# A graph-attention edge pass with each step's relus first on ScalarE, and the projection of step i ahead of the scores of step i-1 on TensorE

## The reference, cut to what matters

```
h = layer_norm(x, ln1_g, ln1_b)
xl, xr = (h @ Wl + bl), (h @ Wr + br)                 # [n, 2 heads, 128]
e = leaky_relu(xl[src] + xr[dst], 0.2)
score = einsum('ehd,hd->eh', e, att)
ex = exp(score - segment_max(score, dst)[dst])
out = segment_sum(xl[src] * (ex / segment_sum(ex, dst)[dst]), dst)
x = x + ((out + gat_b) @ proj_W + proj_b)
h = layer_norm(x, ln2_g, ln2_b)
x = x + (gelu(h @ W1 + b1) @ W2 + b2)
```

## Time and profile before

| | |
|---|---|
| median of three runs | 2266.37 us (2265.63 to 2266.79) |
| span of the profiled execution | 2743.9 us (the page gives no time of this execution beside its span) |
| PE, PE weight loads busy | 72%, 48% |
| DVE, ACT, POOL busy | 47%, 51%, 56% |
| mean granted TensorE clock | 0.891 |

### The profile page before, as it was taken

The page is one execution under the profiler, slowest core; times in us unless marked ns, Lnnn a source line. Parts: engine busy times, 40 slices in busy tenths (PEclk is TensorE's granted clock), DMA queues, the critical chain, the costliest instruction groups (busy, mean ns, idle before and its releaser), DMA issues. The chain is left out here.

```text
span 2743.9 us, 66371 instructions
## 1 busy us (share of the span) xinstructions
PE 1964.3 (72%) x19001; PEld 1307.1 (48%) x19001; DVE 1302.8 (47%) x5318; ACT 1411.6 (51%) x3474; POOL 1543.5 (56%) x1664
## 2 busy tenths in 40 slices
PE   4567777777777777777744777777777777777775
PEld 2234555554554555545533445544545545555453
DVE  7324554554544544544541344444444444444445
ACT  4324555555555555555542455555555555555554
POOL 4656666565566566565315666566556565565540
PEclk9778988989999998998966898999998999889997
DMA  5544444444454454444214444444444444444430
GB/s 133 166 111 127 127 130 128 132 130 128 130 131 128 129 132 129 128 133 128 73 56 117 122 125 128 126 121 129 128 125 128 123 125 127 125 124 128 124 107 7
DMA packets 236750, 332.67 MB, mean 121 GB/s; under 512 B 51011, under 2 KB 160491, under 8 KB 236395
## 3 DMA queue, kind: packets, MB, share of 16 engines
q0 software_dynamic: 75072, 208.30, 29.4%
q1 hardware_dynamic: 161322, 120.16, 14.9%
HBM read 308.02 MB, written 20.25 MB: 120 GB/s over the span
## 5 line engine op out<-in xcount | busy, mean ns | idle before, releaser
L982 POOL DMA_INDIRECT rows<-table,src_t x1564 | 1492.5, 954 | 995.5 <-PE psum L1182 367.9
L1428 DVE SCALAR_TENSOR_TENSOR acc<-acc,keep,psum 128x129 f32 x782 | 273.2, 349 | 1164.2 <-PE psum L1182 596.9
L1207 ACT COPY wgt<-psum 128x256 f32<-128x256 f32 x392 | 146.0, 373 | 1030.2 <-PE psum L1190 649.4
L1089 PE MATMUL psum<-lz,att_w 128*32 128x256 f32 x3128 | 281.2, 434 | 513.6 <-ACT lz L1200 444.6
L1103 PE MATMUL psum<-ident,rows 128*128 128x128 f32 x3128 | 578.4, 315 | 34.9 <-DMA rows<-table,src_t 34.9
L1103 PEld LDWEIGHTS psum<-ident,rows 128*128 128x128 f32 x3128 | 412.3, 160 | 237.5 <-issue 187.8
L1200 ACT ACTIVATE lz<-psum 128x512 f32<-128x512 f32 x782 | 427.8, 603 | 41.0 <-DMA table<-row 14.4
L1182 PE MATMUL psum<-rows,wgt 128*32 128x129 f32 x6256 | 313.8, 302 | 49.3 <-issue 45.9
L1089 PEld LDWEIGHTS psum<-lz,att_w 128*32 128x32 f32 x3128 | 64.4, 113 | 590.0 <-ACT lz L1200 509.4
L1106 PE MATMUL psum<-oh,xrw 96*128 96x256 bf16 x1564 | 344.4, 306 | 0.0
L1279 ACT ACTIVATE ex<-hold_s,peak 128x256 f32<-128x256 f32 x392 | 201.5, 514 | 138.4 <-issue 87.4
(11 more groups left out here) (257 smaller groups left out, 2100.1 us busy)
## 6 DMA issues: line engine op xcount, KB each, us to landing
xrw<-xr_split SPq DMA_DIRECT2D x782, 48.0 KB
relb<-rel_d SPq DMA_DIRECT2D x194, 192.0 KB
rows<-table,src_t POOLq DMA_INDIRECT x1564
relb<-cyc_d SPq DMA_DIRECT2D x194, 64.0 KB
xr_split<-split SPq DMA_DIRECT2D x50, 192.0 KB, 1.9
table<-row SPq DMA_DIRECT2D x50, 130.0 KB, 2.1
x_mid<-x SPq DMA_DIRECT2D x25, 64.0 KB
xo<-x_mid SPq DMA_DIRECT2D x25, 64.0 KB
```

What stands on the lines that cost most here:

```text
L982: pool.indirect_dma_start(rows[:, ring(u), t, u % M, :, :].rearrange("p h c -> p (h c)"), None, s["tables"][layer][0:NP, :], bass.Indirect ...
L1089: m = pe.matmul(out[o:o + W, 0:UE], w["att_w"][:, h * W:h * W + W], lz[:, u % M, h * UE:h * UE + UE], start=False, stop=True, skip_group_c ...
L1428: m = v.scalar_tensor_tensor(a, a, s["keep"][:, u:u + 1], sum_bank(i - 6)[:, c:c + D + 1], ALU.mult, ALU.add)
```

## The change

On ACT, the relus of a step now belong to the units that PE projects in the same step (step i, where it was i-1); they come after the small node work at the head of the step, and ahead of the copy `wgt`, which is now that of step i-4. The exponentials are those of step i-3 and stand ahead of the copy `hold_s`, which is now that of step i-1. On PE, the transposes of `ex` of step i-4 move from the end of the step to its head, `project(i)` comes ahead of `score(i-1)`, and inside `node_work` the combine matmuls (line 1143) come first. The mask product is done in four matmuls of 32 columns where it was two of 64. `lz` has four buffers. DVE's `lowest` is that of step i-2.

```diff
-    lz = sb("lz", [P, M, H * UE], F32)
+    lz = sb("lz", [P, 2 * M, H * UE], F32)
...
                 for u in of_step(g):
-                    at = u % M * HW
-                    pe.matmul(out[at:at + HW, 0:UE], s["mask_w"][:, :], oh[:, u % (3 * M), :],
-                              start=False, stop=False, skip_group_check=True)
+                    for h in range(H):
+                        o = u % M * HW + h * W
+                        pe.matmul(out[o:o + W, 0:UE], s["mask_w"][:, h * W:h * W + W], oh[:, u % (3 * M), :],
+                                  start=False, stop=False, skip_group_check=True)
                 pe.wait_ge(lz_ready, min(g * M + M, NU))
...
-                                      lz[:, u % M, h * UE:h * UE + UE], start=False, stop=True, skip_group_check=True)
+                                      lz[:, u % (2 * M), h * UE:h * UE + UE], start=False, stop=True, skip_group_check=True)
...
             for i in range(END):
+                if of_step(i - 4):
+                    pe.wait_ge(ex_ready, i - 3)
+                    hold(pe, wgt_ready, i - 4)
+                    for t in range(K):
+                        m = pe.transpose(ps[4][:, t * P:t * P + P], ex[:, (i - 4) % 2, t * P:t * P + P],
+                                         s["ident"][:, :])
+                    m.then_inc(ex_turned, 1)
...
+                for u in of_step(i):
+                    project(u)
                 if of_step(i - 1):
                     score(i - 1)
-                for u in of_step(i):
-                    project(u)
                 old = of_step(i - 5)
...
                 node_work(i)
-                if of_step(i - 4):
-                    pe.wait_ge(ex_ready, i - 3)
...
             def relu(u):
 
                 act.wait_ge(z_ready, u + 1)
-                hold(act, score_ready, u // M)
-                act.activation(lz[:, u % M, :], ps[u % M][:, :], ACT.Relu).then_inc(lz_ready, 1)
+                hold(act, score_ready, u // M - 1)
+                act.activation(lz[:, u % (2 * M), :], ps[u % M][:, :], ACT.Relu).then_inc(lz_ready, 1)
 
             for i in range(END):
-                new = of_step(i - 1)
-                if of_step(i - 5):
-                    act.wait_ge(ex_turned, i - 4)
...
-                for u in new:
-                    relu(u)
...
+                for u in of_step(i):
+                    relu(u)
+                if of_step(i - 4):
+                    act.wait_ge(ex_turned, i - 3)
+                    hold(act, sums_ready, i - 5)
+                    act.copy(wgt[:, (i - 4) % 2, :, :].rearrange("p t c -> p (t c)"), ps[4][:, 0:UE]
+                             ).then_inc(wgt_ready, 1)
...
+                old = of_step(i - 3)
+                if old:
+                    n, c = len(old) * HW, (i - 3) % 4
+                    act.wait_ge(max_ready, min(i - 1, NO))
+                    hold(act, ex_turned, i - 4)
...
-                new = of_step(i - 2)
+                new = of_step(i - 1)
                 if new:
                     n = len(new) * HW
-                    act.wait_ge(score_ready, i - 1)
-                    hold(act, ex_ready, i - 5)
...
+                    act.wait_ge(score_ready, i)
+                    hold(act, ex_ready, i - 4)
...
-                if of_step(i - 3):
-                    lowest(i - 3)
+                if of_step(i - 2):
+                    lowest(i - 2)
```

More of the change, by code:

```diff
@@ L1110, in node_work @@
             def node_work(i):
+                for q, tl in [(0, nodes(i, -1)), (1, nodes(i, 0))]:
+                    for t in tl:
+                        pe.wait_ge(staged, t + 1)
+                        if t < NT - 1:
+                            hold(pe, z2_ready if last else xrf_ready, t - 1)
+                        else:
+                            pe.wait_ge(lz_ready, NU)
+                        for m in range(2):
+                            for c in range(3):
+                                mm = pe.matmul(bank(t)[m * HW:m * HW + HW, q * (D + 1):q * (D + 1) + D + 1],
+                                               s["sel"][:, c, :, :].rearrange("p h w -> p (h w)"),
+                                               stg[t % 2][:, 2 * (2 * q + m) + c, :], start=(c == 0),
+                                               stop=(c == 2), skip_group_check=True)
+                        if q == 1:
+                            mm.then_inc(comb_ready, 1)
                 for t in nodes(i, 1):
@@ L1133, in node_work @@
                                   ).then_inc(next_proj, 1)
[L1134 to L1148, removed]
-            for i in range(END):
+            for i in range(END):
+                if of_step(i - 4):
[5 more added lines that the diff above has]
+                    m.then_inc(ex_turned, 1)
                 for t in nodes(i, 5):
@@ L1198, in relu @@
                 act.wait_ge(z_ready, u + 1)
-                hold(act, score_ready, u // M)
-                act.activation(lz[:, u % M, :], ps[u % M][:, :], ACT.Relu).then_inc(lz_ready, 1)
+                hold(act, score_ready, u // M - 1)
+                act.activation(lz[:, u % (2 * M), :], ps[u % M][:, :], ACT.Relu).then_inc(lz_ready, 1)
             for i in range(END):
-                new = of_step(i - 1)
-                if of_step(i - 5):
-                    act.wait_ge(ex_turned, i - 4)
-                    hold(act, sums_ready, i - 6)
-                    act.copy(wgt[:, (i - 5) % 2, :, :].rearrange("p t c -> p (t c)"), ps[4][:, 0:UE]
-                             ).then_inc(wgt_ready, 1)
-                for u in new:
-                    relu(u)
                 for t in nodes(i, 6):
@@ L1267, in _ @@
                     act.activation(am2[:, :], am[t % 2][:, :], ACT.Square).then_inc(sq_ready, 1)
-                new = of_step(i - 2)
+                old = of_step(i - 3)
[3 more added lines that the diff above has]
+                    hold(act, ex_turned, i - 4)
+                    act.activation(ex[0:n, (i - 3) % 2, :], hold_s[0:n, c, :], ACT.Exp, bias=peak[0:n, c:c + 1],
+                                   scale=-1.0).then_inc(ex_ready, 1)
+                new = of_step(i - 1)
                 if new:
                     n = len(new) * HW
-                    act.wait_ge(score_ready, i - 1)
-                    hold(act, ex_ready, i - 5)
[L1273 to L1280, removed]
+                    act.wait_ge(score_ready, i)
+                    hold(act, ex_ready, i - 4)
+                    act.copy(hold_s[0:n, (i - 1) % 4, :], scores(i - 1)[0:n, 0:UE]).then_inc(held, 1)
                 new = of_step(i)
                 if new:
+                    hold(act, score_ready, i - 1)
                     for u in new:
                         act.wait_ge(rows_in[u % ROWS], (u // ROWS + 1) * (16 * K))
-                    hold(act, score_ready, i - 1)
                     act.copy(lin[:, i % 2, :, :].rearrange("p t (c w) -> p (t c) w", w=W),
```

## The result

The changed kernel takes 2208.64 us (median of four runs, 2205.07 to 2211.80) against 2266.58 us of the kernel before: a ratio of 0.9746, with a 95% interval of 0.9729 to 0.9762. The forecast was 2192 us, with POOL's gathers as the bound. The time came out 17 us above the forecast: 58 us were gained where 74 were forecast.

The account below looks back on a forecast made before the run. A loop of waits between PE and ACT bounds the kernel, then POOL's gathers: two passes 1964.5 us plus 221.4 outside make 2185.9, with 3 us a pass for stalls 2192 us; range 2090 to 2255 us.

Parts of the forecast that it names:

- What bounds the kernel: PE and ACT wait for each other: the copy `wgt` stands ahead of the relus, and PE idles 1.00 us a step.
- Which clock to sum by: Span 2743.9 us against median 2266.37: the 477.5 us laid to the profile, so 5.22 us a step from the median.
- The floor: On POOL, gathers follow each other at 1.253 us; four a step make 5.01 us, below which the step cannot go.
- The sum, term by term: Two passes of 982.2 us, 1964.5 together, plus 221.4 outside and 3 us a pass for stalls: 2192 us.
- The mask at no cost: On PE, four 32-column matmuls for two of 64: between nothing and 0.30 us a step, taken as nothing.
- PE's own step of 4.2 to 4.7 us: PE's mean step after the change, without POOL's limit, put below POOL's 5.01 us.
- The wait for `ex` in the table-load step: At the head of PE's step, in one step of eight: 1.0 to 1.3 us, or 0.16 a step.
- Rival 1: New waits of PE for exponentials and POOL for the ring lose part of the gain: 2215 to 2260 us; chance 0.12.
- Rival 2: POOL is not the floor and PE decides: 1986 us, with 1635 to 2142; chance 0.12.
- Rival 3: POOL is the bound already, its interval 1.305 us without a profile: 2262 to 2271 us; chance 0.05.
- Rival 4: PE and ACT take turns at PE's wait for `ex`, step 5.51 us: 2380 us; chance 0.09 with all that is slower.
- The rule on drains: Changing PE's tiling mode drains the engine; two idles, 0.41 and 0.21 us, would go, making PE's step 3.60 us.

Follow-up runs that it names:

- second profile of the kernel before: The kernel before, unchanged, profiled again: 2267.02 us measured, its profiled execution 2267.31 us with a span of 2265.7.
- half of the gathers: The changed kernel with one gather a unit instead of two from unit 20 on (stale rows): 2027.05 us.
- half-gather run of the kernel before: The kernel before with one gather a unit instead of two from unit 20 on: 2256.89 us, against 2265.36 us unedited on one chip.
- two-buffer kernel: The changed kernel with two `lz` buffers instead of four: 3012.15 us on one chip, 2465.95 us on another (ratio 1.0900).
- the kernel with the swap and half of the gathers: The kernel before with only ACT's relus moved ahead of the copy `wgt`, and one gather a unit from unit 20 on: 2027.51 us.

## Why the prediction was right, and where it was off

*What bounds the kernel.* Right: ACT's order closed the loop, and PE's 1.00 us of idle in it is gone. Moving the relus ahead of the copy gives the gain alone.

*Which clock to sum by.* The reason was wrong, the step right. I put the 477.5 us between span and median down to the profile. The second profile of the kernel before has a span of 2265.7 us, and on one of the chips that kernel takes 2749.37 us without a profile. The trace I read fits such an execution: its span and its late starts are those of that chip, though on which chip it was taken is not on record. The 5.22 us a step that I derived from the median instead was close: in the second profile eight steps take 41.8 us (601.9 to 643.7 us by the starts of the copy `wgt`) or 43.4 in pass one and 40.9 in most of pass two, 5.17 in the mean step of both.

*The floor.* Right: where nothing holds them the gathers come at the same distance in both kernels (0.946 us of work and 0.30 between, by the medians of the second profile and of the changed kernel's), and the mask, the buffers and PE's order are covered by it. My four-gather step of 5.01 was 5.04 in the mean. From the last gathers of each pass:

```profile
1079.52 0.95 POOL L982 DMA_INDIRECT rows<-table,src_t  x1 [0.30 <-issue]
...
1154.79 0.97 POOL L982 DMA_INDIRECT rows<-table,src_t  x1 [3.88 <-POOLq L129]
```

and from the last projections:

```profile
1086.63 0.60 PE L1104 MATMUL psum<-ident,rows 128*128 128x128 f32 x4
...
2141.87 0.60 PE L1104 MATMUL psum<-ident,rows 128*128 128x128 f32 x4
```

*The sum, term by term.* First to last gather: 987.2 us (92.3 to 1079.52) and 982.2 us (1154.79 to 2137.0), where I had 978.6 each: 12.2 more, of which my allowance of 3 us a pass took 6. The mean gather lasts 956 ns (1495.3 us over 1564), not the 946 to 949 of the medians, because a few last 1.1 to 1.6 us; the term of 1.253 us from gather to gather held for a quiet stretch and is 1.261 in the mean. From the last gather to the last projection: 7.1 and 4.9 us where I had 3.65, 4.7 more, because PE was still busy with the step before when the last rows were there. Outside the loops 223.1 us (92.3, 68.2 and 62.6) against 221.4. These add up to the span of 2204.5; 1.7 us more lie between span and time, and 2.5 between that execution and the median.

*The parts.* The mask at no cost: right. PE's own step of 4.2 to 4.7 us: 4.60. The wait for `ex` in the table-load step: right in place, too small in size (3.06 us, not 1.0 to 1.3). In the mean step it is 0.48 us in the changed kernel (187.3 us over 392) and 0.64 with half of the gathers, where I had 0.16, so plain steps wait too. This was the largest error in the parts. I had counted ACT's work from the projections on, but not that DVE's minimum and the step before also come late, nor the lower clock afterwards. POOL covered it: that an error of this size did not show in the time is due to the floor, and not to my estimate of PE's step.

*The rivals.* Rival 1 would need waits for sums; there are none beyond the gap. Rival 2 is the half-gather run, 2027 us, where I had 1986. Rival 3 fell with the half-gather run of the kernel before. Rival 4 exists, two `lz` buffers away. One of my own signs of being wrong, PE's largest wait being the one for `ex`, came close: 187.3 us against 208.6 for rows.

*The rule on drains.* The sums follow the attention product without the idle of the earlier trace rows; for the mask the two timelines show 0.22 us a step. But the step of 3.60 us that I gave by it did not come: it is 4.60, of which 0.64 are the wait for `ex`. How much the other width changes take was not tried.

## What to carry to other kernels

When two engines wait for each other in each step, look for the one instruction that stands ahead of a ready one in an engine's order; moving it may be all that is needed, and it is worth trying before the larger reordering, which here cost 121 us by itself where nothing covered it. Work out the next floor first: here the loop had 230 us to give and the gathers let 58 through. And when a profiled span and the measured median differ by a fifth, profile again before any number is taken from it.

## What the runs showed of the hardware that was not expected

On one chip the kernel before takes 2741 to 2752 us in seven runs, on two others 2261 to 2271 in fourteen and 2265 to 2269 in seven, with the same program. In the first, as in the earlier trace rows, ACT, DVE, POOL and SP start late after PE's work is done. There the two-buffer kernel takes 3012 us where it takes 2466 on the other. But the kernel with the swap and half of the gathers takes 2027.5 there, just what the changed one with half of the gathers takes elsewhere; its profile has such late starts only near the start of each pass, while all gathers still run:

```profile
ACT lz L1200 <- remote: 23.6, 4, 10.7
```

So on that chip the delay goes with the gathers: the traces show it while all of them run, and hardly otherwise. Why, and what the change is worth there, stays open: the changed kernel itself was not run on it.
